# The start of a state-space and mixture-of-experts kernel: a gate in another buffer, statistics in the setup, eight weight buffers, and 64 slots laid out by TensorE's work

## The reference

```python
x = L0_attn_x                                   # (4, 2048, 512) float32
mod = (_silu(L0_c) @ L0_wmod).reshape(4, 6, 1, 512)   # sa, ca, ga, sb, cb, gb
h = _layernorm(x) * (1 + ca) + sa
z = h @ W_in;  val, gate = split(z)             # _mamba_fwd(h)
val = silu(depthwise_conv3(val))
B, C = val @ W_B, val @ W_C                     # 16 states
Delta = softplus((val @ W_delta + delta_base) @ W_tau)
dA = Delta[..., None] * -exp(A_log)
# over the tokens: h_t = exp(dA) * h_t-1 + expm1(dA)/(dA + 1e-6) * Delta * B * val ; y_t = sum_n h_t * C
out = (y * silu(gate)) @ W_out + h
x = x + ga * out
h = _layernorm(x) * (1 + cb) + sb
x = x + gb * moe(h)      # 8 experts, the best two, and a shared one: gelu(h @ W1 + b1) @ W2 + b2
```

## Time and profile before

| | |
|---|---|
| median of three runs | 4633.78 us |
| the profiled execution's own time | 4627.73 us |
| its span | 4625.9 us |
| DVE busy | 4041.7 us, 87% |
| ACT busy | 3897.0 us, 84% |
| PE busy | 3854.2 us, 83% |
| POOL busy | 3537.2 us, 76% |
| mean granted TensorE clock | 0.897 |

### The profile page before, as it was taken

The page is one execution under the profiler, slowest core; times in us unless marked ns, Lnnn a source line. Parts: engine busy times, 40 slices in busy tenths (PEclk is TensorE's granted clock), DMA queues, the critical chain, the costliest instruction groups (busy, mean ns, idle before and its releaser), DMA issues.

```text
span 4625.9 us, 36850 instructions
## 1 busy us (share of the span) xinstructions
PE 3854.2 (83%) x9708; PEld 1610.8 (35%) x9708; DVE 4041.7 (87%) x3895; ACT 3897.0 (84%) x4224; POOL 3537.2 (76%) x2240
## 2 busy tenths in 40 slices
PE   7445344998998999999989999998999987989989
PEld 3112112333333333333343433333333333433444
DVE  1688989999999999999999999999999999879720
ACT  3788988998989898998989898989989898988811
POOL 0489887787878888887879888887889787867621
PEclk8666666998999999999999999999999998989889
DMA  4388887787888889888888888898888887756641
GB/s 158 111 270 254 249 242 211 224 250 226 246 251 240 251 240 270 227 254 248 237 259 238 255 237 262 239 265 225 257 252 238 234 229 202 204 157 187 167 138 52
DMA packets 352602, 1036.11 MB, mean 224 GB/s; under 512 B 41253, under 2 KB 44389, under 8 KB 345222
## 3 DMA queue, kind: packets, MB, share of 16 engines
q1 hardware_dynamic: 278666, 765.30, 47.5%
q0 software_dynamic: 73728, 268.47, 29.5%
HBM read 638.69 MB, written 126.51 MB: 165 GB/s over the span
## 4 chain that ended last, share of the span: by engine, by line
ACT 23%; PE 22%; issue 16%; POOL 13%; DMA 13%; DVE 12%; SPq 0%; POOLq 0%; DVEq 0%; ACTq 0%
DMA ysum<-hs 12%; PE ps L1095 7%; PE ps L1118 5%; ACT inv L690 4%; PE ps L1060 4%; POOL inv L1371 3%; POOL hs L1344 3%; ACT th L701 3%; ACT inv L683 3%; ACT abar L705 2%; DVE ps L1158 2%; DVE ps L1164 2%; ACT inv L696 2%; DVE ps L1152 2%; POOL ysum L1358 2%
## 5 line engine op out<-in xcount | busy, mean ns | idle before, releaser
L1371 POOL TENSOR_TENSOR inv<-inv,th 128x1024 f32<-128x1024 f32 x512 | 1261.3, 2463 | 183.7 <-ACT th L701 181.6
L1095 PE MATMUL ps<-hf,w1r 128*128 128x512 f32 x2304 | 1121.4, 639 | 72.9 <-ACT hid L810 42.7
L1344 POOL TENSOR_TENSOR hs<-hs,Cb 128x1024 f32<-128x1024 f32 x384 | 964.1, 2511 | 49.8 <-DVE hs L1182 32.8
L1152 DVE SCALAR_TENSOR_TENSOR ps<-ps,us 128x1024 f32<-128x1024 f32 x512 | 628.4, 1227 | 207.1 <-PE ps L1135 206.8
L1135 PE MATMUL ps<-Brow,pick 48*128 48x512 bf16 x1024 | 337.6, 413 | 489.7 <-DVE hs L1182 488.6
L1358 POOL DMA_DIRECT2D ysum<-hs x480 | 428.9, 894 | 398.5 <-DMA ysum<-hs 373.9
L683 ACT ACTIVATE inv<-delta,minus_pole 128x1024 f32<-128x1024 f32 (+1 forms) x640 | 578.0, 968 | 175.9 <-DVE ps L1164 175.7
L1118 PE MATMUL ps<-w2r,hid 128*128 128x512 f32 x1584 | 723.3, 602 | 0.0
L1171 DVE SCALAR_TENSOR_TENSOR ps<-delta,minus_pole,ps 128x1024 f32<-128x1024 f32 (+1 forms) x640 | 675.1, 1073 | 15.7
L1182 DVE TENSOR_TENSOR_SCAN hs<-abar,carry,ps 128x512 f32<-128x512 f32 (+1 forms) x384 | 683.4, 1801 | 0.4
L1095 PEld LDWEIGHTS ps<-hf,w1r 128*128 128x128 f32 x2304 | 453.3, 203 | 657.6 <-issue 570.9
(11 more groups left out here) (163 smaller groups left out, 4902.7 us busy)
## 6 DMA issues: line engine op xcount, KB each, us to landing
ysum<-hs POOLq DMA_DIRECT2D x512, 512.0 KB, 5.6
Cb<-c_rows SPq DMA_DIRECT2D x384, 512.0 KB, 4.6
w1r<-in_W SPq DMA_DIRECT2D x144, 512.0 KB, 5.4
w2r<-w_scaled SPq DMA_DIRECT2D x129, 512.0 KB, 7.7
Cb<-c_rows SPq DMA_DIRECT2D x128, 256.0 KB, 4.4
gbc<-expert_gates SPq DMA_DIRECT2D x128, 256.0 KB, 5.2
xa<-in_x SPq DMA_DIRECT2D x32, 512.0 KB, 7.3
aw<-in_W_val SPq DMA_DIRECT2D x64, 256.0 KB, 6.1
```

Of the source, the lines that this page charges most:

```text
L1095: mm = t.matmul(o, w1r[:, n % 2, k, h * P:(h + 1) * P], hf[:, k, :], start=(k == 0), stop=(k == G - 1))
L1152: v.scalar_tensor_tensor(X(c), X(c), 1.0, us[:, u % 2, :], ALU.mult, ALU.mult).then_inc(uB_done, 1)
L1344: gp_.tensor_tensor(hs[:, c % 4, :], hs[:, c % 4, :], Cb[:, c % 2, :], ALU.mult).then_inc(hC_done, 1)
L1371: gp_.tensor_tensor(inv[:, c % 6, :], inv[:, c % 6, :], th[:, c % 3, :], ALU.mult).then_inc(thinv_done, 1)
```

## The change

- `gate` of block 0 goes to the buffer of W1 and W_out (`wout`) instead of `xa`, so `load_x` of block 1 waits only for block 0's transposes (`mm_t`) and is issued in the setup.
- Block 1's statistics (DVE) and its normalization (ACT) stand in the setup.
- On PE the four `mod` jobs stand ahead of the four gate jobs; the DVE work on the mod rows is in the setup too, with `signs` and `mags` in `x1`. The gate jobs follow the broadcasts of slots 0, 1 and 2.
- `aw` has eight buffers; the steps at which SP loads them change accordingly, for all blocks.
- Slots 4 to 63 take steps -36 to 63, not evenly but by `front_begins_at`: a step counts 3.8 plus its PE jobs' costs. PE's jobs are given out in pieces of single matmuls between broadcasts (`pe_in_pieces`), as the last blocks' jobs already were.

```diff
-    AWB = 5
+    AWB = 8
+        def gate_of(q):
+            return wout if q == 0 else xa[:]
...
-        signs = w1r[:, 0].rearrange("p k h -> p (k h)").rearrange("p (m d) -> p m d", m=2)
-        mags = w1r[:, 1].rearrange("p k h -> p (k h)").rearrange("p (m d) -> p m d", m=2)
+        signs, mags = x1[:, 0:2, :], x1[:, 2:4, :]
...
-        PACE = [(-12, 0, -44, -44), (0, 2 * WIN, -44, 2 * WIN), (2 * WIN, (NQ - 2) * WIN, ...
+        FRONT_FROM, FRONT_AT, FRONT_TO = 4, -36, 2 * WIN
+        PACE = [(-12, FRONT_FROM, FRONT_AT, FRONT_AT), (2 * WIN, (NQ - 2) * WIN, ...
...
+        def front_begins_at(v):
+            time = [3.8 + sum(PE_COST[j[0]] for j in pe_jobs(*divmod(n, WIN))) for n in range(FRONT_AT, FRONT_TO)]
+            stored = FRONT_TO - 15 - FRONT_AT
+            i = int(v - FRONT_AT)
+            done = sum(time[:i]) + ((v - FRONT_AT - i) * time[i] if i < len(time) else 0)
+            first, total = sum(time[:stored]), sum(time)
+            if i < stored:
+                return FRONT_FROM + (FRONT_TO - 9 - FRONT_FROM) * done / first
+            return FRONT_TO - 9 + 9 * (done - first) / (total - first)
+
         def share(t, behind=0.0):
+            if FRONT_FROM <= t < FRONT_TO:
+                return [v for v in range(FRONT_AT, FRONT_TO) if min(int(front_begins_at(v) + behind), FRONT_TO - 1) == t]
...
         def load_x(sp, q, part):
-            ge(sp, st_gate, 16 * q)
+            if q == 1:
+                sp.wait_ge(mm_t, G)
+            else:
+                ge(sp, st_gate, 16 * q)
...
-            if r == 0:
-                load_aw(sp, qa, 5)
-                load_aw(sp, qa, 6)
-            if r == 1:
-                load_aw(sp, qa, 7)
-            if r == 2:
-                load_aw(sp, qa, 8)
+            if r in (1, 3):
+                for j in range(AWB + r - 1, AWB + r + 1):
+                    load_aw(sp, qa, j)
...
-            if r == 8:
-                load_aw(sp, qa, 9)
-                load_aw(sp, qa, 10)
-            if r == 9:
-                load_aw(sp, qa, 11)
...
             if r == 11:
-                for j in range(AWB - 2):
+                for j in range(G):
                     load_aw(sp, qn, j)
             if r == 20:
-                for j in range(AWB - 2, AWB):
+                for j in range(G, AWB):
                     load_aw(sp, qn, j)
...
-                if batch == -1 and place == "half logs":
+                if batch == -1 and place == 3:
                     act_steps(act, -2, 1, 3)          # gate 0 and 1 out of PSUM
-                if batch == -1 and place == 0:
+                if batch == 0 and place == "squared":
                     act_steps(act, -2, 2, "half logs")   # gate 2 and 3
-                if batch == -1 and place == 3:
+                if batch == 0 and place == 3:
                     act_steps(act, -2, 3, "start")       # silu of the gate
...
+            for part in range(2):                        # sync_opening
+                load_x(sp, 1, part)
...
+            for w in (4, 5, 6):                          # act_opening: normalize block 1
+                for place in PLACES:
+                    act_steps(act, -2, w, place)
...
-            for r in range(20):                          # pe_opening
+            for r in range(11):
                 run(-2, r)
             pe.wait_ge(ld_rest, 96)
+            pe_slot(pe, -1)
+            pe_slot(pe, 0)
+            run(-2, 11)
+            pe_slot(pe, 1)
+            run(-2, 12)
+            pe_slot(pe, 2)
+            run(-2, 13)
...
+            dve_steps(dve, -2, 16)                       # dve_opening
+            dve_steps(dve, -2, 17)
             dve.wait_ge(tau_done, 1)
             for r in (9, 10):
                 dve_steps(dve, -2, r)
             dve_steps(dve, -2, 11, True)
+            other_mod_rows(dve)
```

More of the change, by code:

```diff
@@ L363, in adaln_mamba_moe @@
         PART_TIME = [(FIRST_STEPS if v < WIN else STEP_TIME)[v % WIN] for v in range(3 * WIN)]
-        PE_COST = {"w1": 3.6, "w2": 5.4, "out": 4.7, "t2": 0.9, "log": 7.0, "gT": 1.0}
+        PE_COST = {"t": 1.8, "val": 4.8, "gate": 4.8, "p": 4.8, "bc": 4.8, "mod": 3.8, "modT": 2.0, "w1": 3.6, "w2": 5.4, "out": 4.7, "t2": 0.9, "log": 7.0, "gT": 1.0}
         ACT_BEHIND, DVE_BEHIND, POOL_BEHIND = 0.3, 0.6, 0.3
@@ L928, in pe_jobs @@
                 table.update({7: [("p", qa, 0), ("p", qa, 1)], 8: [("p", qa, 2), ("p", qa, 3)], 9: [("bc", qa, 0)],
[L929 to L930 removed]
+                              10: [("mod", qa, i) for i in range(len(LATER_MODS))], 11: [("gate", qa, 0), ("gate", qa, 1)],
+                              12: [("gate", qa, 2)], 13: [("gate", qa, 3)], 28: [("modT", qa, 0), ("t", qn, 0), ("t", qn, 1)]})
             if H >= NQ - 1:
@@ L936, in bank_held_to @@
             kind, q, i = j
-            start = WIN * (q - 3) if kind == "t" else WIN * (q - 2) if kind in ("val", "gate", "p", "bc", "mod", "modT") else WIN * (q + 2)
+            start = WIN * (q - 3) if kind == "t" else WIN * (q - 2) if kind in ("val", "gate", "p", "bc") else WIN * (q + 2)
             if kind in ("w2", "out"):
                 return at + 1.95
+            if q == 0 and kind in ("bc", "mod", "gate", "modT"):
+                return WIN * (q - 2) + {"bc": (12,), "mod": (12.1, 12.2, 12.3, 12.4), "gate": (27, 27.1, 27.2, 27.3), "modT": (28.3,)}[kind][i]
             held = {"t": (29.2, 29.3, 30.1, 30.2), "val": (1.5, 2.5, 3.5, 3.9), "gate": (8.3, 8.4, 9.5, 9.6), "p": (10.9, 11, 11.4, 11.5),
-                    "bc": (14.6,), "mod": (24.3, 24.4, 24.5, 24.6), "modT": (29,), "t2": (12, 12.1, 12.6, 12.7), "log": (14.95,), "gT": (15.9,),
+                    "bc": (14.6,), "t2": (12, 12.1, 12.6, 12.7), "log": (14.95,), "gT": (15.9,),
                     "w1": (15.4, 15.5, 15.9, 16.3, 17, 17.2, 19.4, 19.5, 20.6, 20.7, 21, 21.1, 25.1, 25.2, 25.8, 25.9,
@@ L980, in taken, with pe_in_pieces @@
             return ev_w2, 12 * q + i + 1
-        PIECES = {"w1": G, "w2": 3 * HT, "out": G + 1, "t2": 1, "log": TPB, "gT": 1}
-        def pe_last_parts(pe):
-            slot = LAST
+        PIECES = {"t": 1, "val": G, "gate": G, "p": G, "bc": G, "mod": 1, "modT": 1, "w1": G, "w2": 3 * HT, "out": G + 1, "t2": 1, "log": TPB, "gT": 1}
+        def pe_in_pieces(pe, first, until, v0, v1, begin_of):
+            slot = first
             pe_slot(pe, slot)
-            for v in range(LAST, LAST + 3 * WIN):
+            for v in range(v0, v1):
                 jobs = pe_jobs(*divmod(v, WIN))
-                begin, length = begins_at(v), begins_at(v + 1) - begins_at(v)
+                begin, length = begin_of(v), begin_of(v + 1) - begin_of(v)
                 total, done = sum(PE_COST[j[0]] for j in jobs), 0.0
@@ L996, in pe_last_parts @@
                         done += PE_COST[j[0]] / PIECES[j[0]]
-            for slot in range(slot + 1, NQ * WIN):
+            for slot in range(slot + 1, until):
                 pe_slot(pe, slot)
@@ L1500, in sync_opening_end @@
         def sync_opening_end(sp):
-            store_gate(sp, 0)
-            for j in range(AWB - 2):
+            for j in range(G):
                 load_aw(sp, 1, j)
-            for part in range(2):
-                load_x(sp, 1, part)
         def act_opening(act):
@@ L1685, in _ @@
                     sync_slot(sp, t)
+                    if t == 4:
+                        for j in range(G, AWB):
+                            load_aw(sp, 1, j)
+                    if t == 6:
+                        store_gate(sp, 0)
                     for H, r in steps_of(t):
```

43 lines of the change are left out of this document (24 added, 19 removed).

## The result

Four runs of the changed kernel took 4580.48 to 4587.96 us, median 4584.31; four of the kernel before, beside them, 4631.63 to 4638.03, median 4635.42. The ratio is 0.9895, 95% interval 0.9884 to 0.9907: 1.05% faster. The forecast was 4565 in a range of 4540 to 4595; the direction and the range hold, the size is 19 us short. The profiled execution took 4587.09 us with a span of 4585.3, so it is 40.6 us shorter than the one before, not 69.

What follows compares the result with a forecast made beforehand. DVE's scan slots set the clock, held up by waits for x and PE, with POOL limiting the middle. Savings of 38.7, 10.3, 15 and 5 us sum to 69, taken from the median 4633.78: 4565 us, range 4540 to 4595.

Steps and rivals of the forecast that it cites:

- Setup: Up to scan 0: without the wait for x of block 1, scan 0 starts at 119.5 us, 38.7 us saved.
- Slots 0 to 4: A broadcast wait and the mod rows leave, ACT waits 3 to 6 us for gate 3; 10.3 us saved (9 to 14).
- Slots 5 to 53: Eight weight buffers and short pieces of PE work between broadcasts: 15 us saved, ends 0 and 35.
- So PE should hold up DVE no more: Slots 5 to 53: six matmuls, 7.5 us, fit between broadcasts, so 49.5 us of DVE waits on PE would go.
- POOL as the limit of the middle: Slots 5 to 53: POOL needs 422 to 446 us, so only 11 to 35 us can be saved.
- DVE waiting for `inv`: Sign from slot 5 on: DVE waits for POOL's inv instead of for PE, with POOL at 8.7 us a slot or more.
- Slots 54 to 63: No folds there, and one 5.2 us wait for a broadcast behind val jobs goes: 5 us saved (3 to 6).
- Slots 64 on: Same engine lists, only SP's weight loads differ: 0 us, with 3 us either way.
- the prediction's own test, 3879 within 5: The prediction is wrong if scan 64 to the end is not 3879 us within 5.
- Slower by the low clock: Rival, 3%: PE's pieces stay at the low clock, 84 us of new stalls in 21 slots; 4669 us, or 4640.
- The middle gives nothing: Rival, 18%: setup and slots 0 to 4 give 49 us, the rest 0 to 5, because of POOL, ACT and DMA; 4580 to 4587.
- 35 + 6 us in the middle: Rival, 12%: the middle gives all it can, 35 + 6 us; 4539 us.

Runs made afterwards that it cites:

- e9: The changed kernel run once more, unchanged, on the same chip as three other versions; median 4577.3 us, ratio to the kernel before 0.9889.
- e7: The changed kernel with POOL's fold multiplications cut to 32 of 512 columns; median 4571.2 us, ratio to the kernel before 0.9869.
- e4: The changed kernel with the same layout of steps but whole jobs, never cut by a broadcast; median 4589.6 us, ratio to the kernel before 0.9913.
- e1: The changed kernel with steps spread evenly over slots 4 to 63 and whole jobs; median 4595.2 us, ratio to the kernel before 0.9924.
- e2: The kernel before with eight weight buffers and the changed kernel's load steps, nothing else; median 4625.9 us, ratio to before 0.9991.
- e3: The changed kernel with five weight buffers and the load steps of before; median 4569.2 us, ratio to the kernel before 0.9870.
- e5: e3 with more room in the pacing for three kinds of step and modulation columns copied one step earlier; median 4563.3 us, ratio to before 0.9850.
- e11: The kernel of e5 run once more, beside a repeat of the changed kernel; median 4561.4 us, ratio to the kernel before 0.9862.

## Why the prediction was right in direction and too hopeful in size

- **Setup (38.7 forecast, 34.1 found): right.** The steps behind the first Abs came out to 0.1 us. The start of that Abs moves from run to run with the clock of PE early in the setup: over the ten other profiles with this setup scan 0 lies between 119.6 and 124.9 us, and at 121.5 in the repeat of the changed kernel, e9. In the stretch from 29 to 43 us the granted clock is 1.00 where scan 0 is at 119.6 to 120.3 (six profiles), 0.88 where it is at 121.4 and 121.5 (two), and 0.76 where it is at 124.1 to 124.9 (three, the profiled changed kernel among them). In those six the setup is 38.0 to 38.7 us shorter than before, as forecast: the term missed by a state of the clock that the profile before didn't have, and not by its chain. The 38.7 was worked out for one start; e7, whose Abs began 0.2 us from before's 99.34, has scan 0 at 119.7.
- **Slots 0 to 4 (10.3, found 13.2): right, with one term too large.** ACT waited 1.66 us for gate 3, not 3 to 6, and lost 0.6 us in slots 0 to 4, not 3.5. Counted from scan 0, ACT was ready after 12.3 us (forecast 12.5), and gate 3 after 13.9, not 15.5 to 18.5: its job began right behind the broadcast that scan 1 freed and took 3.70 us, the high level. Scan 5 is at 161.2 (forecast 159), late by the setup.
- **Slots 5 to 53 (15, found 3.8): the mis-sized term.** The step that failed is "So PE should hold up DVE no more". It counted how long six matmuls take, which was right (the clock is 0.69, e4 prices the pieces at 7 us), and not what the first of them waits for: 30.1 us of broadcasts remain, because the job ahead waits for ACT or for DVE. Nor did it ask how far apart the steps without PE jobs would lie, which made the 20.8 us for x. The layout by PE's work, which made them, gave nothing in return (e4 against e1). The eight buffers' share was sound: in e2, with the old pacing, they give 16.7 us, about the term's whole size, and the waits for `w_delta_tau` went as said. In the changed kernel they have no such work to do, as e3 shows.
- **POOL as the limit of the middle: wrong for this kernel, right for the next one.** The sign named, DVE waiting for `inv`, is absent after, and e7 gives 12 us where this reasoning had the whole stretch hang on POOL. With the new waits taken out (e5, e11) POOL shows up, with 22.5 us of such waits at 441 us, which is inside the 422 to 446 that was worked out. The forecast had 457 - 15 = 442 for the stretch; that is where e5 and e11 are.
- **Slots 54 to 63 (5, found -0.9).** The 5.2 us at slot 63 are gone, and 5.5 us for x at slot 55 stand in their place: the same missing step.
- **Slots 64 on (0 within 3, found 9.6 longer): wrong.** By the prediction's own test, 3879 within 5, this failed; the repeat e9, 4.6 longer, lies within it. "DVE does not wait for them before, so I count 0" looked only at who waits for the weights, not at what else their loads hold up: DVE's waits for `inv` rose from 5.1 to 11.8 us. Another 4.6 of the 9.6 are the edge columns' operation (13.9 us against 9.2), and these come and go: in e9 it has 4.0.
- **The rivals.** Slower by the low clock: refuted, 0.69 against 0.68. By the Trainium skill, "TensorE: Matmul & The Clock Gate", section on HAM oscillation, groups separated by waits begin slow. The trace agrees for what follows idle time (at 174 us two rows take 2.05 us behind 8.05 us of waiting, and the broadcasts behind them 0.52 each). Pieces that follow other matmuls are no such groups: at 185 us (timeline of PE, below) ten rows take 4.56 us, 0.46 each, which is the high level, though two broadcasts cut them off from the piece before. *The middle gives nothing* has the right number, 4580 to 4587, by another cause: not POOL and DMA at once in the stalls' place, but two waits that the new spacing makes. Two sums of the rivals don't come out: 35 + 6 us in the middle, in place of 20, give 4544 and not 4539, and 84 us of stalls with POOL's 35 beneath give 4634 and not 4640. And PE's share and clock are low in the second to the seventh slice, not the first six. The range stays as it was by either.

```profile
184.56 0.60 PE L1155 MATMUL ps<-Brow,pick 48*128 48x512 bf16 x2
185.09 4.56 PE L1045 MATMUL ps<-hT,aw 128*128 128x512 f32 x10
189.58 0.60 PE L1155 MATMUL ps<-Brow,pick 48*128 48x512 bf16 x2
```

In sum, -34.1 - 13.2 - 3.8 + 0.9 + 9.6 = -40.6 us: of the 28.4 us between that and 69, the middle has 11.2, the steady part 9.6, slots 54 to 63 5.9, the setup's start 4.6, and slots 0 to 4 give 2.9 back. Some 10 of the 28.4 come from which two executions were profiled: by the medians the kernel is 19 us short of the forecast.

## What to carry to other kernels

When a planner spaces steps by one engine's work, look at the steps in which that engine has none: they fall together, and a store, a load and its first reader may lie closer than a DMA takes. In a list in order, the length of what stands ahead of an instruction is only half of its delay; ask for each job what it waits for, and place it behind that, or its wait is handed to all behind it. And a deeper buffer is worth what the present spacing makes it wait: price it again once the spacing has changed.

## What the runs showed of the hardware that was not expected

One tiny operation of DVE, the edge columns of `uu` (L1310, 128x8), is as a rule 0.17 us and took up to 5.23. Its sixteen executions in the changed kernel (ns, min/median/max) are

```profile
L1310 DVE TENSOR_TENSOR uu<-uu,vhalo x16: 163/166/5227, 72.8 to 3557.8; 128x8 f32<-128x8 f32 x16
```

The timeline of DVE and POOL around the longest says what it waits for:

```profile
1756.53 5.23 DVE L1310 TENSOR_TENSOR uu<-uu,vhalo 128x8 f32<-128x8 f32 x1
1756.79 2.63 POOL L1362 TENSOR_TENSOR hs<-hs,Cb 128x1024 f32<-128x1024 f32 x1
1759.10 2.61 POOL L1389 TENSOR_TENSOR inv<-inv,th 128x1024 f32<-128x1024 f32 x1
1761.68 1.22 DVE L1184 SCALAR_TENSOR_TENSOR ps<-ps,inv 128x1024 f32<-128x1024 f32 x1
```

It ends at 1761.76, 0.05 us after the second of two POOL products that follow each other (1761.71). In the profiles of before, after and e9 this operation has 14 executions over 0.3 us, and each ends 0.03 to 0.05 us after a POOL product; the other 34 take 0.16 to 0.17 us, and no POOL product runs beside them. A POOL DMA issue beside it doesn't lengthen it (1237.24 us in e9). Its two inputs both lie in SBUF, the engines' main buffer, as do those of the other operation that behaves so, the `w2r` product of 9x512 (L1211), 0.68 us alone and up to 2.67; `times_u`, which has one input in PSUM, takes 1.21 to 1.23 us in all its 512 executions, whatever POOL does. That the place of the inputs makes the difference is an inference from these three operations; no run moved one of them. So a tiny DVE operation can cost as much as POOL has in hand, and no wait shows it: the time counts as DVE's busy time. Which products it meets differs from run to run, and with them the operation's sum from slot 64 on, from 4.0 us (e9) to 13.9 (after).
